# TensorE as four 64x64 arrays in three of the four passes of a two-layer cross convolution

## The reference

```
wI  = w + eye(16)
ret = x @ wI
hq  = x . qw1[t]  (2 values);  ret += hq @ qw2[t];  ret += x * qdd[t]     # depends on the row t only
hk  = x . kw1[s]  (2 values);  ret += hk @ kw2[s];  ret += x * kdd[s]     # depends on the column s only
```

## Time and profile before

| | |
|---|---|
| median of 3 runs | 987.24 us (987.24 to 987.75) |
| profiled execution, its own time | 987.69 us |
| its span, first to last instruction | 985.8 us |
| mean granted TensorE clock | 0.986 |
| TensorE busy, share of the span | 96% |
| DVE, ACT, POOL busy | 76%, 32%, 73% |
| HBM read, written | 89.2 MB, 69.3 MB |

### The profile page before, as it was taken

One profiled execution on the slowest core, in us unless ns is written; L12 is line 12 of the kernel. 1 busy time (PEld: TensorE's weight loads), 2 busy tenths in 40 slices (PEclk: granted clock), 3 DMA queues, 4 the chain that ended last, 5 costly groups with the idle time before them and its releaser, 6 DMA issues.

```text
span 985.8 us, 24446 instructions
## 1 busy us (share of the span) xinstructions
PE 946.6 (96%) x8378; PEld 939.4 (95%) x8378; DVE 748.4 (76%) x1036; ACT 319.2 (32%) x514; POOL 715.7 (73%) x603
## 2 busy tenths in 40 slices
PE   3679999999999999999999999999999999999998
PEld 3669999999999999999999999999999999999998
DVE  3996767787777876788677886779767786778997
ACT  0234333323333333333333233333333333333320
POOL 2998876678766976669866787668876697665666
PEclk8789999999999999999999999999999999999999
DMA  8952118770386506872088702866048730784017
GB/s 214 328 142 61 16 47 296 258 185 1 129 292 240 125 1 210 287 245 43 1 288 288 202 6 86 282 253 164 1 167 286 255 73 1 243 293 128 1 44 299
DMA packets 76493, 159.74 MB, mean 162 GB/s; under 512 B 39936, under 2 KB 40960, under 8 KB 73856
## 3 DMA queue, kind: packets, MB, share of 16 engines
q1 hardware_dynamic: 76416, 158.54, 50.5%
HBM read 89.19 MB, written 69.34 MB: 161 GB/s over the span
## 4 chain that ended last, share of the span: by engine, by line
PE 88%; POOL 7%; DMA 2%; issue 2%; POOLq 1%; DVE 0%
PE PB L482 24%; PE PA L482 23%; PE PA L488 21%; PE PB L488 20%; POOL WA L160 3%; POOL PROD L265 2%; DMA RT<-products 2%; POOL PROD L269 1%; DMA products<-RT 1%; POOL PROD L272 0%; DVE WA L448 0%; POOLq L288 0%; POOLq L160 0%; DVE RT L375 0%; POOLq L283 0%
## 5 line engine op out<-in xcount | busy, mean ns | idle before, releaser
L160 POOL TENSOR_TENSOR WA<-RT,mask 128x512 f32<-128x512 f32 x277 | 341.9, 1242 | 151.1 <-PE PA L482 121.2
L160 POOL TENSOR_TENSOR WA<-RS,mask 128x512 f32<-128x512 f32 x256 | 328.2, 1292 | 104.8 <-PE PA L488 87.3
L482 PE MATMUL PA<-X,WA 128*128 128x128 f32 x2048 | 281.9, 280 | 26.4 <-POOL WA L160 19.5
L482 PEld LDWEIGHTS PA<-X,WA 128*128 128x128 f32 x2048 | 257.2, 192 | 31.5 <-issue 23.9
L405 DVE TENSOR_TENSOR OUT<-PB,X 128x512 f32<-128x512 f32 x256 | 176.0, 691 | 131.2 <-PE PB L482 130.0
L488 PE MATMUL PA<-Y,WA 128*128 128x128 f32 x2048 | 267.9, 272 | 5.9 <-POOL WA L160 5.9
L488 PE MATMUL PB<-X,WB 128*128 128x128 f32 x2048 | 267.5, 272 | 0.0
L338 ACT ACTIVATE Y<-PA 128x512 f32<-128x512 f32 (+1 forms) x256 | 162.1, 633 | 321.6 <-PE PA L482 321.6
L344 ACT ACTIVATE X<-PA 128x512 f32 x256 | 155.6, 608 | 311.1 <-PE PA L488 311.1
L488 PEld LDWEIGHTS PA<-Y,WA 128*128 128x128 f32 x2048 | 247.2, 188 | 7.3 <-POOL WA L160 7.2
L482 PE MATMUL PB<-Y,WB 128*128 128x128 f32 x1880 | 250.3, 274 | 0.0
...
## 6 DMA issues: line engine op xcount, KB each, us to landing
X<-in_x_dram SPq DMA_DIRECT2D x128, 512.0 KB, 4.9
out_dram<-OUT SPq DMA_DIRECT2D x128, 512.0 KB, 3.1
RT<-products SPq DMA_DIRECT2D x16, 1024.0 KB, 11.8
OUT<-in_right_dram SPq DMA_DIRECT2D x2, 1024.0 KB, 11.0
products<-PROD SPq DMA_DIRECT2D x16, 128.0 KB, 4.1
Y<-in_right_dram SPq DMA_DIRECT2D x1, 1024.0 KB, 22.9
X<-in_right_dram SPq DMA_DIRECT2D x1, 1024.0 KB, 26.8
...
```

The source lines that it names most:

```text
L160: engine.tensor_tensor(dst, r, m, ALU.mult).then_inc(ready, 1)
L482: last = nc.tensor.matmul(bank[:, r, :], weights[:, r].rearrange("q n p -> q (n p)"), row(buf, pair, r), start=True, stop=True)
```

## The change

TensorE works as four 64x64 arrays in t1, s1 and s2: an array is chosen by the half of the input partitions and the half of the output partitions. The partitions are now ordered part before channel, so that 64 of them hold 4 parts with all 16 channels, and the matrices are block diagonal with 4 blocks of 16 in 64x64. t1 sends the two halves of the columns of each half of the partitions to different output halves; its copies put them in Y so that s1 and s2 find a layout of their own (s1 adds in it), and s2 brings them back. t2 stays whole, 128x128.

- t1: a group is a chunk of 8 rows, 32 matmuls of 64x64 with 64 columns into two banks; two ACT copies. One 128x512 weight tile holds all 8 rows' matrices (before: 4 rows).
- s1, s2: a group is 4 column indices of each half, 16 matmuls of 64x64 with 128 columns into two banks; s1 has two DVE adds, s2 three ACT copies (one whole, two of 64 partitions). There are 16 groups for each pass and block.
- t2: 32 groups of 4 matmuls in 4 banks, one DVE add each, as before. A row phase alternates two groups of t2 (8 rows) and one of t1 (8 rows).
- Weight tiles: of s1 and t2 DVE builds the even, POOL the odd groups; of t1 and s2 POOL builds all. Per block: POOL 16 + 16 + 8 + 16 (before 64), DVE 8 + 16 (before 64).
- The rings in PSUM of t1, s1, s2 have two places of two banks each.
- The compact row matrices (`row_matrices`, 8 operations a block) move from POOL to DVE, after chunk 6 of the row phase, and their two stores on SP to after chunk 9 of the row phase.
- Start: the column factors are loaded once for 8 partitions, repeated over the partitions by matmuls with a selection matrix (`fill`) into PSUM, multiplied and added from there by DVE (`column_unit`, 16 times two operations), onto a base that ACT makes with 32 activations. The first block's row matrices come as 32 rows and then 96. `warm_up` is gone.

The core of the diff:

```diff
-SPLIT = P // CH
...
-COLS = S // SPLIT
+HALVES = 2
+HALF = P // HALVES
+PARTS = HALF // CH
+EIGHTHS = HALVES * PARTS
+COLS = S // EIGHTHS
+WIDE = COLS // HALVES
...
-GRP = 4
-GROUPS = ROWS // GRP
-RING = 4
-LAG = 2
+PAIRS = ROWS // PAIR
...
-PER_CHUNK = CHUNK // GRP
...
+NARROW = 4
+GROUPS = WIDE // NARROW
+INDEX = HALVES * NARROW
+FEW = 4
+FEW2 = FEW // PAIR
+PER_CHUNK = CHUNK // FEW
+T2_GROUPS = ROWS // FEW
+RING = 2
 SLOTS = 4
+OUT_SLOTS = 4
+LAG = 2
+QUARTERS = 4
+QUARTER = COLS // QUARTERS
+UNITS = LAYERS * QUARTERS * RANK
+FILLS = 4
+FIRST_ROWS = 32
+PROD_STEP = 6
+PROD_STORE = 9
...
-DVE_T2 = [g for g in range(GROUPS) if g < RING or g % 4 == 1]
-POOL_T2 = [g for g in range(GROUPS) if g not in DVE_T2]
...
+        def spread_quarter(engine, dst, compact, ready):
+            shape = [P, CHUNK, PARTS, CH]
+            r = compact.unsqueeze(2).broadcast_to(shape)
+            m = mask[:, :].unsqueeze(1).unsqueeze(3).broadcast_to(shape)
+            engine.tensor_tensor(dst.rearrange("q (t a n) -> q t a n", t=CHUNK, a=PARTS), r, m, ALU.mult
...
+        def spread_whole(engine, dst, compact, ready):
+            shape = [P, FEW, EIGHTHS, CH]
+            r = compact.unsqueeze(2).broadcast_to(shape)
+            m = mask8[:, :].unsqueeze(1).unsqueeze(3).broadcast_to(shape)
+            engine.tensor_tensor(dst.rearrange("q (t p n) -> q t p n", t=FEW, p=EIGHTHS), r, m, ALU.mult
...
+                load_rows(LAYERS * k + 1, 1, 0, ROWS, rt_loaded[1])
                 if more:
-                    sp.wait_ge(wa_ready, before_s2(k))
-                    load_rt(k, 0)
-                    sp.wait_ge(prod_ready, LAYERS * (k + 2))
-                    for l in range(LAYERS):
-                        store_products(k + 1, l, PROD[:, l, 0], prod_stored)
+                    sp.wait_ge(wa_ready, s2_groups(k))
+                    load_rows(LAYERS * k, 0, 0, ROWS, rt_loaded[0])
...
+                    if more and o == PROD_STORE:
+                        sp.wait_ge(prod_ready, LAYERS * (k + 2))
+                        for l in range(LAYERS):
+                            store_products(LAYERS * (k + 1) + l, PROD[:, l, 0], prod_stored)
+                        if params:
+                            load_q(k + 2)
...
+            load_rows(BLOCKS * LAYERS, 0, 0, FIRST_ROWS, rt_first)
             load_x(0, 2)
-            load_x(0, 3)
-            for h in range(2):
-                load_right(KR1[h], 1, h, right_loaded[1 + h])
-            for j in range(4, CHUNKS):
+            load_rows(BLOCKS * LAYERS, 0, FIRST_ROWS, ROWS - FIRST_ROWS, rt_loaded[0])
+            for j in range(3, CHUNKS):
...
+            def s_phase(k, more):
+                for step in range(GROUPS + LAG):
+                    ahead = step + SLOTS
+                    if step % 2 and step < GROUPS:
+                        if ahead < GROUPS:
+                            s1_matrices(k, ahead)
+                        else:
+                            t2_matrices(k, ahead - GROUPS)
+                    ahead = step - LAG + SLOTS
+                    if step >= LAG:
+                        if ahead < GROUPS:
+                            s2_matrices(k, ahead)
+                        elif more:
+                            t1_matrices(k + 1, ahead - GROUPS)
+            def t_phase(k, more):
+                for o in range(CHUNKS):
+                    ahead = PER_CHUNK * o + 1 + SLOTS
+                    if ahead < T2_GROUPS:
+                        t2_matrices(k, ahead)
+                    elif more:
+                        s1_matrices(k + 1, ahead - T2_GROUPS)
+                    ahead = o + SLOTS
+                    if more:
+                        if ahead < CHUNKS:
+                            t1_matrices(k + 1, ahead)
+                        else:
+                            s2_matrices(k + 1, ahead - CHUNKS)
...
+            def t1_copies(k, j):
+                act.wait_ge(a_full, t1_groups(k) + j + 1)
+                for h in range(HALVES):
+                    nc.scalar.activation(
+                        rows_of(Y, k, j)[:, :, WIDE * h:WIDE * (h + 1), :].rearrange("q a s c -> q a c s"),
+                        PA[HALVES * (j % RING) + h][:, :].rearrange("q (a c s) -> q a c s", a=CHUNK2, c=PAIR),
+                        ACT.Copy).then_inc(a_done, 1)
+            def s2_copies(k, g):
+                lower, upper, every = slice(0, HALF), slice(HALF, P), slice(0, P)
+                act.wait_ge(a_full, s2_groups(k) + g + 1)
+                for i, dst, src in ((0, every, every), (1, lower, upper), (1, upper, lower)):
+                    nc.scalar.activation(columns_of(block_of(X, k), dst, WIDE * i + NARROW * g),
+                                         by_columns(PA[HALVES * (g % RING) + i][src, :]), ACT.Copy
+                                         ).then_inc(a_done, 1)
...
+            def column_unit(u):
+                l, part, i = u // (QUARTERS * RANK), u // RANK % QUARTERS, u % RANK
+                bank = PB[u % FILLS][:, :].rearrange("q (s n) -> q s n", n=CH)
+                at = RS[:, l, QUARTER * part:QUARTER * (part + 1), :]
+                left = KL[:, l, i, QUARTER * part:QUARTER * (part + 1)].unsqueeze(2).broadcast_to([P, QUARTER, CH])
+                dve.wait_ge(right_full, u + 1)
+                chained(nc.vector.tensor_tensor(bank, bank, left, ALU.mult))
+                dve.wait_ge(base_ready, CH * (l + 1))
+                nc.vector.tensor_tensor(at, bank, at, ALU.add).then_inc(right_done, 1)
+                dve.wait_ge(right_done, u + 1)
+            def add_columns(k, g):
+                dve.wait_ge(b_full, s1_groups(k) + g + 1)
+                for h in range(HALVES):
+                    at = columns_of(block_of(Y, k), slice(0, P), WIDE * h + NARROW * g)
+                    nc.vector.tensor_tensor(at, by_columns(PB[HALVES * (g % RING) + h][:, :]), at, ALU.add
+                                            ).then_inc(b_done, 1)
...
+                    add_columns(k, g)
+                    if g % 2 == 0:
+                        ahead = g + SLOTS
+                        if ahead < GROUPS:
+                            s1_weights(nc.vector, ahead, wb_even)
+                        else:
+                            dve.wait_ge(rt_loaded[1], DMA * (k + 1))
+                            t2_weights(nc.vector, ahead - GROUPS, wb_even)
...
+                for o in range(CHUNKS):
+                    add_rows(k, PER_CHUNK * o)
+                    ahead = PER_CHUNK * o + SLOTS
+                    if ahead < T2_GROUPS:
+                        t2_weights(nc.vector, ahead, wb_even)
+                    elif more:
+                        s1_weights(nc.vector, ahead - T2_GROUPS, wb_even)
+                    add_rows(k, PER_CHUNK * o + 1)
+                    if more and o == PROD_STEP:
+                        products_of(k + 1)
...
+                nc.tensor.matmul(PB[u % FILLS][:, :], sel[0:EIGHTHS],
+                                 KR[l][place // per][:, BANK * (place % per):BANK * (place % per + 1)],
+                                 start=True, stop=True).then_inc(right_full, 1)
+            def t1(k, j):
+                pe.wait_ge(x_loaded[j], DMA * (k + 1))
+                pe.wait_ge(wa_ready, t1_groups(k) + j + 1)
+                if j >= RING:
+                    pe.wait_ge(a_done, t1_done(k) + T1_COPIES * (j - RING + 1))
+                elif k:
+                    pe.wait_ge(a_done, t1_done(k) - S2_COPIES * (RING - 1 - j))
+                for r in range(CHUNK):
+                    for h in range(HALVES):
+                        for o in range(HALVES):
+                            last = nc.tensor.matmul(
+                                PA[HALVES * (j % RING) + h][part(o), WIDE * r:WIDE * (r + 1)],
+                                matrix(WA[:, j % SLOTS], h, r),
+                                rows_of(X, k, j)[part(h), r // PAIR, WIDE * o:WIDE * (o + 1), r % PAIR],
+                                start=True, stop=True)
+                last.then_inc(a_full, 1)
...
+            def s1(k, g):
...
+                for v in range(NARROW):
+                    for h in range(HALVES):
+                        for o in range(HALVES):
+                            last = nc.tensor.matmul(
+                                PB[HALVES * (g % RING) + h][part(o), ROWS * v:ROWS * (v + 1)]
+                                .rearrange("q (a c) -> q a c", c=PAIR),
+                                matrix(WB[:, g % SLOTS], h, NARROW * o + v),
+                                column(X, k, h, WIDE * o + NARROW * g + v), start=True, stop=True)
+                last.then_inc(b_full, 1)
...
+            def s2(k, g):
...
+                for v in range(NARROW):
+                    for h in range(HALVES):
+                        for i in range(HALVES):
+                            last = nc.tensor.matmul(
+                                PA[HALVES * (g % RING) + i][part(h ^ i), ROWS * v:ROWS * (v + 1)]
```

(11 more changed lines are left out.)

560 lines of the change are left out of this document (253 added, 307 removed).

## The result

The changed kernel takes **860.6 us** (median of 4 runs, 856.45 to 869.87) against 987.32 us before: a ratio of 0.8702, 95% interval 0.8665 to 0.8739. It is faster, as predicted, but by 127 us where 279 were forecast, and 860.6 lies above the range of 655 to 815. The profiled execution took 858.88 us, span 857.1.

A forecast was written before the change was run, and what follows sets the result against it. The prediction took TensorE, busy 96% of 985.8 us, to bound the kernel. Start 48, eight column phases of 33, seven row phases of 51 and a last of 37 gave 706 us, plus 1.9 outside: 708, range 655 to 815.

The forecast's parts named there:

- the 33: Column phase: 16 steps at POOL's 1.94 us make 31 us, the start adds about 2; bounds 30 and 40.
- The first rival: Tiled row pass: a 64-column pair costs 27 ns like a 128-column one, 798 us in all; chance 0.04.
- The second rival: Column passes: reads of pairs 1 KB apart halve the arrays' pace, column phase stays at 58, total 908 us; chance 0.06.
- The third: Small-array passes: arrays sharing input rows run one after the other, 57 ns a pair, total 1006 us; chance 0.05.
- I take 27 ns there too: Column passes: pairs of elements a row apart keep the warm-up's 27 ns a pair, 1.71 us of TensorE a step.
- The bound of 57: Column passes: 57 ns a pair, arrays working two at a time, kept as the other end to 27 ns.
- the high end of 40: Column phase: upper bound of 40 us, each wait between four balanced engines costing a tenth more.
- The two stores of products that move here add some 3: Row phase: the moved products' stores, 4.1 us to landing each, add some 3 us to 43 us of DMA.
- the floor of 46 us by DMA: Row phase: DMA's 43 us for the same 15 MB plus some 3 for products' stores, below TensorE's 51 us.
- The low bound: Row phase: 46 us, set by the DMA floor, under the forecast of 51 us; the high bound was 58.
- a row phase over 58 says that a change of size costs twice my price: Row phase sign: over 58 us means an array-size change costs twice the 0.21 us priced, two changes a chunk.
- so does a first row pass at the lower clock level, since x binds: Start: a first row pass at the lower clock hides behind x loads; first column phase at 48 us, bounds 43 and 60.

The follow-up runs named there:

- e1: Changed kernel with both column passes reading 128 neighbouring elements of constant tile RS instead of pairs 1 KB apart; 838.33 us in one run.
- e2: Changed kernel with PAIR 4 instead of 2, so column reads take four neighbouring elements and row reads one in four; 1092.34 us.
- e15: Changed kernel with row-matrix loads of one row from the second block on, and a quarter of x (from the third block) and output moved; 788.58 us.
- e16: e15 with the column passes also reading 128 neighbouring elements; 746.42 us in one run.
- e7: Changed kernel with products stored as 128 packets of 1 KB instead of 2048 of 64 bytes, same bytes; 839.54 us in one run.
- e9: Changed kernel with products built by DVE and stored in the column phase again, as before the change; 841.93 us.
- e4: Changed kernel with 14 whole-array matmuls between the first four fills and the first t1; 865.71 us, ratio 0.8737.

## Why the prediction was wrong

**Right: the mechanism and its sizes.** Four arrays work side by side; a pair of 64 columns takes 15.1 ns where 14.5 was taken (64 of them in a group of 0.95 us); a chunk 3.12 us for 3.17 and a row phase without traffic 50.5 for 51; the last row phase 35.3 for 37. With contiguous reads a column phase is 33.7 for 33, but this is in part luck: the 33 had POOL bind at 1.94 us a step, 31 in all, and POOL was busy for 28.0 of the 33.7 us there and TensorE for 30.8; POOL binds nowhere. The first rival, a floor per small matmul, is out: 15.1 ns over whole groups and not 27. By the Trainium skill (TensorE: Matmul & The Clock Gate, "Wait — 56ns, not 53.3ns?") starts never come closer than about 25 ns; the 15.1 disagrees. The second rival, column reads, named the right place, but a pair takes a third longer (36 ns for 27) and not twice as long. The third, arrays with common input rows one after the other (57 ns a pair), is out too: 36 ns at worst, 27 with contiguous reads.

**Wrong:**

1. *"They did so on contiguous or every-second-element columns ...; I take 27 ns there too."* The pair of columns read 1 KB apart costs 36 ns, so TensorE and not POOL binds the column phase: 39.5 us for 33, 8 x 6.5 = 52 us. The bound of 57 was named, but the high end of 40 for the phase was worked out from waits between engines, not from it; that 39.5 lies below it is luck. e1, e2, e15 and e16 show it.
3. *"The two stores of products that move here add some 3"* and the floor of 46 us by DMA: the row phase was taken as TensorE's with DMA at 0.9 beside it. Waits for x (25 us), stops (19) and lost clock (some 14, an estimate) overlap in part and made 54 us; x took 6.0 us to land for 4.9 before, a products' store 8.2 for 4.1. 25 of the 54 go with the products' small packets (e7) and 39 with the products' leaving the row phase (e9). The low bound was seen, the queueing below saturation was not. The prediction's own sign misled here: "a row phase over 58 says that a change of size costs twice my price", but four phases are over 58 and the two changes cost 0.34 us a chunk for 0.42.
4. *The start: "so does a first row pass at the lower clock level, since x binds."* x does not bind, no matmul waits for it before 70 us. TensorE does: 3.9 us a chunk at 1.2 GHz. Of these 2.0 are a `fill`, for which the sum had DVE's time and none of TensorE's. Twelve make 24 us; without them the first column phase would begin near 46 even at the lower level, where 48 was forecast (an estimate; no run leaves the fills out). A warm-up ahead of it was no cure (e4). +22 us.

The parts: 22 + 52 + 28.4 (the rest of the column phases) + 54 - 3.5 (row phases' own pace) - 1.7 = 151 us, the miss. The 28.4 is what is left of these phases' 80.4, so the sum closes by itself; their stops, 21.7, and the clock lost in them, about 7 by the clock column, come to 28.7.
